# Ternary feed-forward weights prepared in the last batch's attention, and the last pairs' ends interleaved with the first feed-forward rows

## The chip, the cores and the metric

The kernel runs on one core of one Trainium2 chip. The metric is device time in microseconds (us) of one execution. The engines are PE (TensorE, matmuls), DVE (VectorE), ACT (ScalarE), POOL (GpSimd) and SP (SyncE, which here issues all DMAs). Each engine works through its own instructions in order; between engines only semaphores order the work.

## The reference

A transformer layer in fp32: differential attention after a layer norm, then a feed-forward block with ternary weights after a second layer norm, both with a residual. Batch 8, sequence 1024, width 512, 16 heads of 32, hidden width 2048.

```python
x = x + attn(layernorm(x))
# attn: q, k, v = (x @ w_qkv) in 16 heads of 32, q and k split into halves of 16
a = softmax(q1 k1 * s) - lam * softmax(q2 k2 * s)
out = rmsnorm(a @ v) * norm_w * 0.2          # then reshaped (heads * seq, 32) -> transposed -> (seq, 512)
return out @ wo

x = x + ffn(layernorm(x))
def bitlinear(x, w):                          # ffn
    scale = clip(mean(abs(w), axis=1), 1e-5)
    tern = clip(round(w / scale), -1, 1)
    return x @ (tern * scale).T
h = bitlinear(x, w_fc) + gate * (x @ v.T @ fast_b.T @ u.T)
return bitlinear(relu(h) ** 2, w_proj)
```

## The kernel before

**Attention.** Work goes by pairs of heads: 8 batches of 8 pairs, P = 0 to 63 (`NPAIR`). A pair has 16 tiles, 8 for each of the two softmaxes (j = 0, 1), and one turn of the inner loop (d = 0 to 7) handles two tiles. For a tile PE computes scores in two halves (`pe_score`, L530, PSUM banks 0-1 and 2-3), ACT takes the exponential of each (`act_exp`, L863) into a ring of four tiles `pr`, PE multiplies them with V (`pe_pv`, L557), and DVE adds the tile to `acc` (`dve_add`, L1156, none for the first tile of each eight). A half's scores wait for the exponential of the same half one tile before; an exponential waits until the tile four before it is added and multiplied. `pe_sum` (L574) turns `acc` into row sums; ACT makes their inverse with a logarithm and an exponential (`act_sum_ln` L869, `act_sum_exp` L873).

**Ends of pairs.** What is left of a pair after its tiles is cut into steps (`pe_post`, `act_post`, `dve_post`, `sync_post`), which ride along with the next three pairs: step 1 `ot` (DVE L1169, L1172), 2 its square (ACT), 3 the mean square by matmul into bank 5 (PE L589, `rms`), 4 its inverse root (ACT L889, L892) and `on` (DVE L1179), 7 transposes and their split `oth`, `otl` (PE L599, ACT L897, DVE L1183), 13 the load of the pair's rows of x into `xr` (SP L353), 14 and 15 twelve matmuls with `wo` into bank 7 (PE L610), 16 the addition `xr` (DVE L1188) and its write to `x2_scratch` (SP L357). There is one `xr`: the load of a pair's rows waits until the pair before has been written.

**Projections.** While batch b attends, the matmuls `x @ w_qkv` of a later batch run in pieces within its pairs (`pe_tile`, L469). For the last batch, pairs 56 to 63, nothing is left to project.

**Seam.** After pair 63 the ends of the last three pairs run down (loops such as L413, L775, L977 and L1303). Then, when the last rows are written (`s_x2` at 16 x 64), the feed-forward weights are prepared in eight slices, four of `w_fc` and four of `w_proj`. For each slice: SP loads 1 MB into `wf` (three slots; the first three loads are issued at the end of pair 55), ACT sums magnitudes (`act_magnitudes`, L908), DVE forms scales and compares against plus and minus half a scale (`dve_ternary`, L1205 to L1219) into `tt`, PE transposes 16 blocks through all eight banks (`pe_ternary`, L683), ACT copies them into `tT` or `tP` (`act_ternary`, L916). Between slices 4 and 5 the low-rank weights `w2s` are formed from `u`, `fast_b` and `v` (L1310 to L1337, `pe_low_rank_weights` L692 to L707, with 32-row casts L1333 and L1331). Then follow the layer norm of the first 512 rows (`dve_ln_step`, L1033 to L1055), the row of projection scales `prow` (PE L794, DVE L1349), the transposes of the rows (`pe_turn_rows` L661, ACT L922, DVE L1385), and `pe_low_rank` (L669).

**Feed-forward.** 16 blocks of 512 rows, 16 steps in each: `pe_up` (L629, L634), ACT relu (L1009), DVE square (L1360), ACT rounding (L1014), DVE remainder (L1362), `pe_down` (L644).

**Order.** The order on every engine is written out by hand. SBUF: in the seam, buffers of the feed-forward lie over those of attention, which is why its work starts after the last pair.

Of the kernel before, what the change touches and what calls it, by code (L numbers as in the profile page):

```python
# [31 lines left out]
STG = 8  # L32
# [12 lines left out]

def tile_of(m):
    return 2 * m if m < 4 else 2 * (m - 4) + 1
# [19 lines left out]
def build(nc, x, wqkv, wo, lq1, lq2, lk1, lk2, norm_w, fast_b, w_fc, w_proj, u, v, gate, out):  # L67
# [6 lines left out]
    with ExitStack() as top:  # L74
# [12 lines left out]
        scp = sbuf(top, "scp", [128, 4, 4])  # L87
        eps5, eps6, neglam, gatec = small[:, 0:1], small[:, 1:2], small[:, 2:3], small[:, 3:4]
        dt_ = small[:, 8:16]

        g1 = top.enter_context(ExitStack())
        with ExitStack() as al:
            wf = sbuf(al, "wf", [128, 3, HID])
            ta = sbuf(al, "ta", [128, 2, HID])
        wqh = sbuf(g1, "wqh", [128, 4, 3 * E], FR)
        wql = sbuf(g1, "wql", [128, 4, 3 * E], FR)
        woh = sbuf(g1, "woh", [128, 4, E], FR)
        wol = sbuf(g1, "wol", [128, 4, E], FR)
# [29 lines left out]
        with ExitStack() as al:  # L128
            pr = sbuf(al, "pr", [128, NPB, 2, 2, 512])
        with ExitStack() as al:  # L130
            wst = sbuf(al, "wst", [128, 4, 3 * E])
        with ExitStack() as al:
            stp = sbuf(al, "stp", [128, STG, 2, 512], FR)
        wos = acc[:, 0, :].rearrange("p (k n) -> p k n", k=4)
        g1.close()

        g2 = top.enter_context(ExitStack())
        with ExitStack() as al:
            zt = sbuf(al, "zt", [128, 2, 512], FR)
            zq = sbuf(al, "zq", [128, 512], FR)  # L140
            rb = sbuf(al, "rb", [128, 2, 512])
            sb2 = sbuf(al, "sb2", [128, 2, 512])
            hh_ = sbuf(al, "hh_", [128, 3, 512], FR)
            hl_ = sbuf(al, "hl_", [128, 3, 512], FR)
            fo = sbuf(al, "fo", [128, 4, E])
        sbuf(g2, "wf_place", [128, 3, HID])
        sbuf(g2, "ta_place", [128, 2, HID])
        tT = sbuf(g2, "tT", [128, 4, HID], FR)
        tP = sbuf(g2, "tP", [128, 16, E], FR)
        w2s = sbuf(g2, "w2s", [128, HID], FR)  # L150
        vth = sbuf(g2, "vth", [128, 4, 128], FR)
        vtl = sbuf(g2, "vtl", [128, 4, 128], FR)
        prow = sbuf(g2, "prow", [128, E])
        x2 = sbuf(g2, "x2", [128, 2, 4, E])
        xn = sbuf(g2, "xn", [128, 4, E])
        mv2 = sbuf(g2, "mv2", [128, 4, 2])
        st62 = sbuf(g2, "st62", [128, 4, 6])
        rs2 = sbuf(g2, "rs2", [128, 16])
        ln2 = sbuf(g2, "ln2", [128, 24])
        with ExitStack() as al:  # L160
            tt = sbuf(al, "tt", [128, 2, HID])
            us = sbuf(al, "us", [128, 16, RANK])
            ut = sbuf(al, "ut", [128, 2, 128])
            fba = sbuf(al, "fba", [128, 128])
            fbm = sbuf(al, "fbm", [128, 8, 128])
            vrep = sbuf(al, "vrep", [128, E])
            w2t = sbuf(al, "w2t", [128, 512], FR)
            dg = sbuf(al, "dg", [128, 4, 128])
            on1 = sbuf(al, "on1", [128, 128])
        with ExitStack() as al:  # L170
            yh = sbuf(al, "yh", [128, 2, 4, 512], FR)
            yl = sbuf(al, "yl", [128, 2, 4, 512], FR)
# [1262 lines left out]
```

## Time and profile before

| | |
|---|---|
| time, median of 3 runs | 4001.5 us (3999.47 to 4004.07) |
| profiled execution | 4001.55 us, span 3999.8 us |
| busy in the span | PE 3826.3 us (96%), DVE 3197.0 (80%), ACT 2834.5 (71%), POOL 2.0 |
| granted PE clock, whole execution | 0.987 |
| chain that ended last, by engine | PE 79%, DVE 10%, ACT 6%, issue 3%, DMA 1%, SP queue 1% |

The page shows the span in 40 slices of 100 us. PE, ACT and DVE are at nine, eight and nine tenths from the second slice on; slice 29 has PE and DVE at eight, ACT at four and the clock at six tenths; from slice 30 on PE is at nine, DVE at five, ACT at three. The tables of the page and the answers of the trace are read for where an engine idles and what ended its wait, since a busy share alone is an average over stages.

### The profile page before, as it was taken

To read this page: it belongs to the slowest core of one execution; us is meant where nothing else is said; L and a number is where in the kernel's file an instruction comes from. 1 tells how busy PE (TensorE), PEld (TensorE's weight loads), DVE (VectorE), ACT (ScalarE), POOL (GpSimd) and SP (SyncE) were. 2 spreads that over 40 slices of the span, in tenths; PEclk is the share of its full clock that TensorE was granted. 3 is DMA by queue.
4 is the path that set the end of the run, shared out by engine and by line. 5 is a ranking of instruction groups with operands and counts; after the bars stand their busy time and mean duration, and the time that the engine had idled before them with its cause. 6 is when DMAs were issued, how large, how long until landed. Compare 5 with 4: busy or idle time off the path is not lost.

```text
span 3999.8 us, 57643 instructions
## 1 busy us (share of the span) xinstructions
PE 3826.3 (96%) x22088; PEld 2113.7 (53%) x22088; DVE 3197.0 (80%) x3030; ACT 2834.5 (71%) x3573; POOL 2.0 (0%) x14
## 2 busy tenths in 40 slices
PE   6799999999999999999999999888499999999999
PEld 5344444444444444444444444232378787878887
DVE  5699999999999999999999999999655555555554
ACT  2688888888888888888888888888433333333333
POOL 0000000000000000000000000000000000000000
PEclk9899999999999999999999999999699999999999
DMA  5445444454454444444444545331201010101010
GB/s 196 123 100 117 101 111 111 94 124 98 111 109 100 115 108 109 107 104 110 107 111 103 111 97 125 63 67 38 90 6 38 22 42 22 43 22 43 22 43 22
DMA packets 225844, 338.25 MB, mean 85 GB/s; under 512 B 86704, under 2 KB 107184, under 8 KB 225008
## 3 DMA queue, kind: packets, MB, share of 16 engines
q1 hardware_dynamic: 225520, 333.88, 34.4%
q8 instruction: 210, 3.44, 0.4%
q14 instruction: 114, 0.93, 0.1%
HBM read 180.72 MB, written 150.99 MB: 83 GB/s over the span
## 4 chain that ended last, share of the span: by engine, by line
PE 79%; DVE 10%; ACT 6%; issue 3%; DMA 1%; SPq 1%; DVEq 0%; ACTq 0%
PE ps L557 18%; PE ps L530 13%; PE ps L629 12%; PE ps L644 12%; DVE acc L1156 7%; PE ps L469 7%; PE ps L472 5%; PE ps L610 4%; ACT pr L863 4%; PE ps L574 3%; PE ps L634 2%; PE ps L589 1%; PE ps L445 1%; PE ps L669 1%; PE ps L661 1%
## 5 line engine op out<-in xcount | busy, mean ns | idle before, releaser
L863 ACT ACTIVATE pr<-ps 128x1024 f32<-128x1024 f32 x2048 | 1983.9, 1027 | 248.8 <-PE ps L530 244.2
L1156 DVE TENSOR_TENSOR acc<-acc,pr 128x2048 f32<-128x2048 f32 x768 | 1755.4, 2286 | 55.2 <-ACT pr L863 27.8
L557 PE MATMUL ps<-pr,vst 128*32 128x512 f32 x8192 | 1021.2, 600 | 0.0
L530 PE MATMUL ps<-qst,kst 50*128 50x512 f32 x4096 | 786.0, 456 | 55.4 <-ACT pr L863 37.8
L530 PEld LDWEIGHTS ps<-qst,kst 50*128 50x128 f32 x4096 | 329.7, 184 | 721.7 <-ACT pr L863 534.6
L1009 ACT ACTIVATE rb<-ps,scf 128x512 f32<-128x512 f32 x256 | 175.9, 687 | 407.1 <-PE ps L634 407.1
L557 PEld LDWEIGHTS ps<-pr,vst 128*32 128x32 f32 x8192 | 207.9, 109 | 439.9 <-issue 429.8
L629 PE MATMUL ps<-yh,tT 128*128 128x512 f32 x1024 | 410.4, 401 | 0.0
L644 PE MATMUL ps<-tP,hh_ 128*128 128x512 f32 x1024 | 406.2, 397 | 1.9 <-DVE hl_ L1362 1.9
L629 PE MATMUL ps<-yl,tT 128*128 128x512 f32 x1024 | 405.3, 396 | 0.0
L1360 DVE TENSOR_TENSOR sb<-rb 128x512 f32<-128x512 f32 x256 | 176.9, 691 | 282.9 <-ACT rb L1009 281.6
L644 PE MATMUL ps<-tP,hl_ 128*128 128x512 f32 x1024 | 401.2, 392 | 0.0
L1156 DVE TENSOR_TENSOR acc<-pr 128x2048 f32<-128x2048 f32 x128 | 293.0, 2289 | 104.4 <-ACT pr L863 104.4
L1362 DVE TENSOR_TENSOR hl_<-sb,hh_ 128x512 fp32r<-128x512 f32 x256 | 177.2, 692 | 178.9 <-ACT hh_ L1014 178.9
L1014 ACT ACTIVATE hh_<-sb 128x512 fp32r<-128x512 f32 x256 | 162.0, 633 | 202.5 <-DVE sb L1360 202.5
L469 PE MATMUL ps<-xth,wqh 128*128 128x512 f32 x512 | 223.1, 436 | 9.7 <-DVE stg L1089 9.7
L644 PEld LDWEIGHTS ps<-tP,hh_ 128*128 128x128 f32 x1024 | 192.3, 188 | 60.4 <-DVE fo L1396 12.5
L629 PEld LDWEIGHTS ps<-yh,tT 128*128 128x128 f32 x1024 | 192.6, 188 | 43.2
L629 PEld LDWEIGHTS ps<-yl,tT 128*128 128x128 f32 x1024 | 192.6, 188 | 42.9
L644 PEld LDWEIGHTS ps<-tP,hl_ 128*128 128x128 f32 x1024 | 192.3, 188 | 42.8
L469 PE MATMUL ps<-xtl,wqh 128*128 128x512 f32 x512 | 205.9, 402 | 0.0
L469 PE MATMUL ps<-xth,wql 128*128 128x512 f32 x512 | 202.6, 396 | 0.0
(154 smaller groups left out, 3500.8 us busy)
## 6 DMA issues: line engine op xcount, KB each, us to landing
qst<-q_scratch SPq DMA_DIRECT2D x128, 384.0 KB, 6.3
kst<-k_scratch SPq DMA_DIRECT2D x128, 384.0 KB, 9.1
q_scratch<-stg SPq DMA_DIRECT2D x168, 256.0 KB
k_scratch<-stg SPq DMA_DIRECT2D x168, 256.0 KB
xin<-in_L_attn_x_dram SPq DMA_DIRECT2D x16, 1024.0 KB, 5.7
v_scratch<-vsg SPq DMA_DIRECT2D x64, 256.0 KB, 3.0
vst<-v_scratch SPq DMA_DIRECT2D x128, 128.0 KB, 5.5
xr<-in_L_attn_x_dram SPq DMA_DIRECT2D x64, 256.0 KB
```

The costliest lines, as they stand in the source:

```text
L469: t = e.matmul(ps[:, bk, :], w[:, k, m0:m0 + 128], xx[:, k, :], start=(n == 0), stop=(n == 11))
L472: t = e.matmul(ps[:, bk, :], xx[:, k, st * 128:(st + 1) * 128], w[:, k, 2 * E:3 * E], start=(n == 0), stop=(n == 11))
L530: ins = e.matmul(ps[:, 2 * c + hh, :], kst[rows, r, j, t * 128:(t + 1) * 128], qst[rows, r, j, c * 512:(c + 1) * 512], start=True, stop=True)
L557: ins = e.matmul(ps[32 * c4:32 * c4 + 32, 4 + j, :], vst[:, r, t, 32 * hh:32 * hh + 32], pr[:, sl, c, hh, :], start=(t == 0), stop=(t == 7 ...
L629: e.matmul(ps[:, bk, :], tT[:, k, i * 128:(i + 1) * 128], y_[:, bf, k, :], start=(m == 0), stop=False)
L644: t = e.matmul(ps[:, rt, :], h_[:, uu % 3, rt * 128:(rt + 1) * 128], tP[:, i, :], start=(i == 0 and part == 0), stop=(i == 15 and part == 1))
L863: e.activation(pr[:, sl, c, :, :], ps[:, 2 * c:2 * c + 2, :], ACT.Exp, scale=SCALE).then_inc(s_exp, 1)
L1009: e.activation(rb[:, uu % 2, :], ps[:, 4 + uu % 2, :], ACT.Relu, scale=scf[:, 0, i:i + 1]) \
L1014: e.activation(hh_[:, uu % 3, :], sb2[:, uu % 2, :], ACT.Copy).then_inc(s_hh, 1)
L1156: e.tensor_tensor(acc[:, j, :], old, new, ALU.add).then_inc(s_add, 1)
L1360: e.tensor_tensor(sb2[:, uu % 2, :], rb[:, uu % 2, :], rb[:, uu % 2, :], ALU.mult).then_inc(s_sb, 1)
L1362: e.tensor_tensor(hl_[:, uu % 3, :], sb2[:, uu % 2, :], hh_[:, uu % 3, :], ALU.subtract) \
```

## The change

- SBUF is laid out anew. The feed-forward's weights, work buffers and constants (`tT`, `tP`, `tt`, `ta`, `wf`, now with two slots, `us`, `fba`, `vrep`) lie over the projections' buffers (`wqh` to `vsg`), which are free once the last projections are done; the row buffers (`x2`, `xn`) lie over `pr`, `yh` over `acc`, `yl` over `qst`.
- Slice i of the weights is handled in pair 56 + i: magnitudes at d = 0, 2, 3 (ACT), scales and first comparison at d = 4, second comparison at d = 5 and 6 (DVE, two pieces each), transposes and copies at d = 6, 7 and d = 0, 1 of the next pair (PE, ACT), all through bank 6. Every slice is now in four pieces of 512 columns; for `w_proj` a `tensor_reduce` adds the four magnitude sums.
- SP loads slices 0 and 1 at the end of pair 55, `u`, `fast_b` and `v` at d = 1 of pair 56, and one slice at d = 7 of each of pairs 56 to 61. `u` is scaled by DVE at d = 0 of pair 62.
- After pair 63 the order on each engine is written out: the last pairs' ends stand between the low-rank weights, the scales and the layer norm of the first rows. `pe_sum` of the last pair uses bank 3. Rows 0 to 1023 are loaded without waiting for the last batch's writes. ACT rounds all of `w2s` in one instruction a block, so DVE's casts of 96 of the 128 rows go.
- The twelve `wo` matmuls of pair 63 stand in the feed-forward behind its first down step, its addition two steps later.

```diff
@@ SP
+                    if d == 1 and P == NPAIR - NP:
+                        sync_low_rank(e)
+                    if d == 7 and NPAIR - NP <= P < NPAIR - 2:
+                        sync_weights(e, P - (NPAIR - NP) + 2)
                     sync_posts(e, P, d)
-            for d in range(24):
-                sync_posts(e, NPAIR + d // 8, d % 8)
-            e.wait_ge(s_x2, 16 * NPAIR)
...
+            sync_post(e, NPAIR - 3, 16)
             sync_rows(e, 0)
+            sync_post(e, NPAIR - 2, 13)
             sync_rows(e, 1)
...
+            sync_post(e, NPAIR - 2, 16)
+            sync_post(e, NPAIR - 1, 13)
+            sync_post(e, NPAIR - 1, 16)
@@ PE
                     pe_posts(e, P, d)
+                    if last and d >= 6:
+                        pe_ternary(e, P - (NPAIR - NP), d - 6)
+                    if last and d < 2 and P > NPAIR - NP:
+                        pe_ternary(e, P - (NPAIR - NP) - 1, d + 2)
...
+            pe_pv(e, NSLOT - 3)
+            pe_pv(e, NSLOT - 2)
+            pe_ternary(e, 7, 2)
+            pe_pv(e, NSLOT - 1)
+            pe_ternary(e, 7, 3)
+            pe_post(e, NPAIR - 2, 14)
+            pe_post(e, NPAIR - 2, 15)
+            pe_low_rank_factors(e)
+            pe_sum(e, NPAIR - 1, 1)
+            pe_low_rank_weights(e, 0)
+            pe_low_rank_weights(e, 1)
+            pe_row_scales(e)
+            pe_post(e, NPAIR - 1, 3)
+            pe_low_rank_weights(e, 2)
+            pe_low_rank_weights(e, 3)
             for k in range(4):
                 pe_turn_rows(e, 0, k)
+            pe_post(e, NPAIR - 1, 7)
             pe_low_rank(e, 0)
...
+                    if n == 0 and i == 1:
+                        pe_post(e, NPAIR - 1, 14)
+                        pe_post(e, NPAIR - 1, 15)
@@ PE, one transpose bank
+        def pe_ternary(e, i, m):
+            u4 = 4 * i + m
+            e.wait_ge(s_tern, u4 + 1)
+            if u4:
+                e.wait_ge(s_tt, u4)
+            else:
+                tile_read(e, 24 * B - 1)
+            for k in range(4):
+                t = e.transpose(ps[:, 6, k * 128:(k + 1) * 128], tt[:, (4 * m + k) * 128:(4 * m + k + 1) * 128], ident[:])
+            t.then_inc(s_ttr, 1)
@@ ACT
                     act_exp(e, P, k, 0)
+                    if d in (0, 3) and tile >= 0:
+                        act_magnitudes(e, tile, 2 if d else 0)
...
+                    if d in (2, 3) and tile >= 0:
+                        act_magnitudes(e, tile, 2 * d - 3)
                     act_posts(e, P, d, 1)
+                    if d >= 6 and tile >= 0:
+                        act_ternary(e, tile, d - 6)
+                    if d < 2 and tile >= 1:
+                        act_ternary(e, tile - 1, d + 2)
                     act_exp(e, P, k + 1, 1)
@@ DVE
+                        tile = P - (NPAIR - NP)
+                        if tile >= 0 and (d, half) == (4, 0):
+                            dve_ternary_scale(e, tile)
+                        if tile >= 0 and (d, half) in ((5, 1), (6, 0)):
+                            for a in range(2):
+                                dve_ternary(e, tile, 2 * (d - 5) + a)
+                        if tile == 6 and (d, half) == (0, 0):
+                            dve_low_rank_u(e)
                         dve_add(e, P, 2 * d + half)
...
+            dve_post(e, NPAIR - 3, 16, 0)
             e.wait_ge(s_fb, 16 * 12)
+            e.wait_ge(s_pv, NSLOT)
...
+            dve_post(e, NPAIR - 1, 1, 0)
+            dve_post(e, NPAIR - 2, 16, 0)
             e.wait_ge(s_vta, 1)
...
+            dve_low_rank_weights(e, 0)
+            dve_low_rank_weights(e, 1)
+            e.wait_ge(s_w2p, 5)
+            e.tensor_copy(prow[:], ps[:, 1, :]).then_inc(s_prow, 1)
+            for n in range(5):
+                dve_ln_step(e, 2 * B, n)
+            dve_low_rank_weights(e, 2)
+            dve_low_rank_weights(e, 3)
+            dve_post(e, NPAIR - 1, 4, 1)
             for n in range(6, 11):
                 dve_ln_step(e, 2 * B, n)
...
             for k in range(4):
                 dve_turn_rows(e, 0, k)
+            dve_post(e, NPAIR - 1, 7, 1)
             dve_low_rank(e, 0)
```

## Rows read from the trace of the kernel before

**Rows 1.** Busy time by stretch (us): stretch, length, each engine's busy time (instructions), PE clock, DMA.
```profile
2394.81:2436.26 41.45, 41.45 (x266) 18.64 (x264) 39.12 (x27) 36.74 (x44) 0.00 (x0) 1.00 0.49 117
2676.28:2716.08 39.80, 35.71 (x232) 11.88 (x228) 36.18 (x21) 34.48 (x41) 0.00 (x0) 1.00 0.31 62
2812.26:2920.09 107.83, 49.16 (x233) 40.02 (x234) 64.69 (x141) 40.73 (x84) 0.84 (x3) 0.67 0.26 83
2920.09:3992.00 1071.91, 1069.50 (x4708) 857.03 (x4707) 565.87 (x964) 398.80 (x634) 0.00 (x0) 1.00 0.09 29
```

**Rows 2.** Waits in the pair 2676.28 to 2716.08: total us, times, longest.
```profile
DVE acc L1156 <- ACT pr L863: 2.0, 5, 1.1
...
DVE otl L1183 <- ACT oth L897: 0.4, 1, 0.4
...
DVE ot L1169 <- ACT rl L873: 0.2, 1, 0.2
```

**Rows 3.** Order of time in that pair, ACT and PE: start, length (us), engine, line.
```profile
2701.11 3.79 ACT L863 ACTIVATE pr<-ps 128x1024 f32<-128x1024 f32 x4
2705.09 1.94 ACT L863 ACTIVATE pr<-ps 128x1024 f32<-128x1024 f32 x2 [0.20 <-PE ps L530]
2706.37 1.13 PE L589 MATMUL ps<-sq,blk 128*128 128x256 f32 x4
2707.97 1.94 ACT L863 ACTIVATE pr<-ps 128x1024 f32<-128x1024 f32 x2 [0.94 <-PE ps L530]
...
2710.37 1.95 ACT L863 ACTIVATE pr<-ps 128x1024 f32<-128x1024 f32 x2
```

**Rows 4.** Order of time on DVE in the seam, weight preparation and first layer norm.
```profile
2849.19 0.16 DVE L1205 TENSOR_SCALAR scf<-scf 128x4 f32<-128x4 f32 x1
...
2853.90 0.16 DVE L1205 TENSOR_SCALAR scf<-scf 128x4 f32<-128x4 f32 x1
...
2870.52 2.30 DVE L1318 TENSOR_SCALAR us<-us,scf 128x16 f32<-128x16 f32 x16
...
2903.97 2.46 DVE L1033 BATCH_NORM_STATS2 st<-x 128x6 f32<-128x512 f32 x4
...
2908.05 1.92 DVE L1055 TENSOR_SCALAR xn<-x,mv,rs 128x512 f32<-128x512 f32 x4
```

**Rows 5.** Order of time on ACT in the seam, magnitudes and copies.
```profile
2851.24 0.62 ACT L908 ACTIVATE ta<-wf 128x512 f32<-128x512 f32 x1
...
2851.86 2.03 ACT L916 ACTIVATE tT<-ps 128x512 fp32r<-128x512 f32 x4
```

**Rows 6.** Order of time on DVE and SP, end of attention, the last rows' rounds.
```profile
2809.97 2.29 DVE L1156 TENSOR_TENSOR acc<-acc,pr 128x2048 f32<-128x2048 f32 x1 [0.23 <-ACT pr L863]
...
2812.89 0.55 SPq L357 DMA_DIRECT2D x_scratch<-xr  x1
2818.79 0.57 SPq L353 DMA_DIRECT2D xr<-in_L_attn_x_dram  x1
...
2832.24 0.55 SPq L353 DMA_DIRECT2D xr<-in_L_attn_x_dram  x1
...
2837.53 0.69 DVE L1188 TENSOR_TENSOR xr<-ps,xr 128x512 f32<-128x512 f32 x1 [11.18 <-DMA xr<-in_L_attn_x_dram]
...
2844.09 0.17 DVE L1205 TENSOR_SCALAR scf<-scf 128x4 f32<-128x4 f32 x1 [5.87 <-DMA x_scratch<-xr]
```

**Rows 7.** Order of time on PE in the seam, first transposes of weights and rows, the low-rank product.
```profile
2854.04 1.97 PE L683 MATMUL ps<-ident,tt 128*128 128x128 f32 x16 [1.01 <-DVE tt L1219]
...
2910.62 1.76 PE L661 MATMUL ps<-ident,xn 128*128 128x128 f32 x8 [1.91 <-DVE prow L1349]
...
2916.51 0.80 PE L669 MATMUL ps<-yh,vth 128*128 128x512 f32 x1 [1.41 <-DVE yl L1385]
...
2920.09 0.63 PE L629 MATMUL ps<-yh,tT 128*128 128x512 f32 x1
```

**Rows 8.** Line L366, the two loads of 1 MB of rows in the seam.
```profile
DMA to landing us min/median/max: 7.1/8.0/9.0
```

More of the change, by code:

```diff
@@ new lines, in build @@
+            mv2 = sbuf(al, "mv2", [128, 4, 2])
+            st62 = sbuf(al, "st62", [128, 4, 6])
+            rs2 = sbuf(al, "rs2", [128, 16])
+            ln2 = sbuf(al, "ln2", [128, 24])
+        with ExitStack() as al:
+            w2s = sbuf(al, "w2s", [128, HID], FR)
+            zt = sbuf(al, "zt", [128, 2, 512], FR)
+            zq = sbuf(al, "zq", [128, 512], FR)
+            prow = sbuf(al, "prow", [128, E])
+            hh_ = sbuf(al, "hh_", [128, 3, 512], FR)
+            vth = sbuf(al, "vth", [128, 4, 128], FR)
+            hl_ = sbuf(al, "hl_", [128, 3, 512], FR)
+            vtl = sbuf(al, "vtl", [128, 4, 128], FR)
@@ L99, in build @@
+        with ExitStack() as al:
+            wst = sbuf(al, "wst", [128, 4, 3 * E])
+        with ExitStack() as al:
+            stp = sbuf(al, "stp", [128, STG, 2, 512], FR)
+        pr = sbuf(g1, "pr", [128, NPB, 2, 2, 512])
+        acc = sbuf(g1, "acc", [128, 2, 2 * S])
         qst = sbuf(g1, "qst", [128, RING, 2, S], FR)
@@ L183, in build @@
         s_vb = [sem(f"s_vb{k}") for k in range(RING)]
-        s_wf = [sem(f"s_wf{k}") for k in range(3)]
+        s_wf = [sem(f"s_wf{k}") for k in range(2)]
         s_u, s_fb = sem("s_u"), sem("s_fb")
@@ L1224, in build @@
-        dve_count = [0]
+            e.wait_ge(s_abs, 4 * i + 4)
+            if not fc:
+                e.tensor_reduce(scp[:, 3, cols], scq[:, i - 4, :], AX.X, ALU.add).then_inc(s_scl, 1)
+                c += 1
+                e.wait_ge(s_scl, c)
+            e.tensor_scalar(sc[:, 0, cols], sc[:, 3, cols], 1.0 / (512 if fc else 2048), 1e-5, ALU.mult, ALU.max) \
+                .then_inc(s_scl, 1)
+            e.wait_ge(s_scl, c + 1)
+            e.tensor_scalar(sc[:, 1, cols], sc[:, 0, cols], 0.5, None, ALU.mult).then_inc(s_scl, 1)
@@ new lines, in dve_ternary_scale, with dve_ternary @@
+            e.tensor_scalar(sc[:, 2, cols], sc[:, 0, cols], -0.5, None, ALU.mult).then_inc(s_scl, 1)
+            e.wait_ge(s_scl, c + 3)
+            for a in range(4):
+                _, col, cs = wf_part(i, a)
+                e.tensor_scalar(ta[:, cs], wf[:, i % 2, cs], sc[:, 2, col:col + 1], None, ALU.is_lt).then_inc(s_scl, 1)
+        def dve_ternary(e, i, a):
+            sc, col, cs = wf_part(i, a)
+            if i:
+                e.wait_ge(s_ttr, 4 * i)
+            e.wait_ge(s_scl, n_scale(i + 1) - 3 + a)
+            e.scalar_tensor_tensor(out=tt[:, cs], in0=wf[:, i % 2, cs], scalar=sc[:, 1, col:col + 1], in1=ta[:, cs],
+                                   op0=ALU.is_gt, op1=ALU.subtract).then_inc(s_tern, 1)
@@ new lines, in dve_low_rank_u @@
+        def dve_low_rank_u(e):
+            e.wait_ge(s_scl, n_scale(4))
+            e.reciprocal(scf[:, 1, :], scf[:, 0, :]).then_inc(s_lru, 1)
+            e.wait_ge(s_lru, 1)
+            e.wait_ge(s_small, 16 * 9)
+            e.tensor_scalar(scf[:, 2, :], scf[:, 1, :], gatec, None, ALU.mult).then_inc(s_lru, 1)
+            e.wait_ge(s_lru, 2)
+            e.wait_ge(s_u, 16)
+            for t in range(16):
+                ins = e.tensor_scalar(us[:, t, :], us[:, t, :], scf[:, 2, t:t + 1], None, ALU.mult)
+            ins.then_inc(s_w2v, 1)
```

383 lines of the change are left out of this document (154 added, 229 removed).

## Prediction

> **What bounds the kernel now.** I read the page first. Three engines are busy over 70% of the span, so the shares decide nothing, and the slices show what matters: PE, ACT and DVE are dense over 27 slices, thin out in slices 28 and 29, and then PE alone is dense to the end. I then cut the time into stretches [rows 1]. A pair of attention heads with projection matmuls in it takes 41.45 us, and PE is busy for all of it. A pair of the last batch, which has no projections left, takes 39.80 us with PE 35.7, DVE 36.2 and ACT 34.5 busy. The seam from the end of the last addition to `acc` (the addition of 2809.97 lasts 2.29, so it ends at 2812.26 [rows 6]) to the first matmul of the feed-forward (2920.09 [rows 7]) is 107.8 us, with no engine over 60% busy and a granted PE clock of 0.67, a mixture of the 1.2 and the 2.4 GHz level. After it PE is busy 1069.5 of 1071.9 us. So the seam is the loose stretch, the last batch has a little room, and the feed-forward has none: a matmul more there costs its full pitch.
>
> In a last-batch pair no single engine sets the pace. DVE's waits are 2.0 for the exponentials, 0.4 and 0.2 for the ends of earlier pairs, 2.6 us in all [rows 2]. What paces it is the ring between ACT and PE: a half tile of exponentials frees the PSUM banks for the next scores, and the next exponential waits for those. ACT's order of time shows it [rows 3]: two plain tiles take 3.98 us (2701.11 to 2705.09), 1.99 each; the tile with the `rms` matmuls in it takes 2.88, the one with a logarithm 2.40. PE's extra (1.13 us busy, some 1.0 of it added) passes with 0.89 into the period; ACT's extra, about 0.6 us as for any instruction of 512 columns there, with 0.41.
>
> **Part 1: ternary preparation moved into the last eight pairs.** Each pair takes one of eight slices. DVE: in the seam one slice of `w_fc` took from 2849.19 to 2853.90, 4.71 us [rows 4]. A slice of `w_proj` has four pieces now and one small sum more; I take 4.7 for both. ACT: four magnitudes at 0.61 (one starts at 2851.24, what follows at 2851.86) and four copies in 2.03, so 4.5 us [rows 5]. PE: 16 transposes in 1.97 us [rows 7]. What this does to a pair of 39.80:
> - DVE's floor: 39.8 less its waits of 2.6, plus 4.7, is 41.9.
> - ACT's load is 34.5 + 4.5 = 39.0, PE's at most 35.7 + 2.0 = 37.7. Neither is a bound alone.
> - The ring: the transposes stand between two score matmuls, so I pass them on as the `rms` matmuls are (0.89 of 1.97, 1.75 us). Magnitudes pass at ACT's rate (0.41 of 0.6 of 2.46, 1.7 us). The copies stand directly behind transposes, where PE issues the next scores at the same time; that hides them nearly fully (0 to 0.68 x 2.03 = 1.4). The ring is then 43.2 to 44.6.
>
> The bounds: below, the DVE floor (it can't be less, as every piece is issued by DVE in order); above, 44.5, all of DVE's present waits kept and 4.7 added; a ring that hides nothing would give 39.8 + 2.0 + 4.5 = 46.3. I take 43.4, near the low end of the ring since ACT and PE both have 4 us of room, and above the floor: +3.6 a pair, +28.8 over eight. The scaling of the `u` factors, also moved in, is 2.3 us of DVE once [rows 4], and two small instructions ahead of it make it about 2.8; DVE has 43.4 - 41.9 = 1.5 of room by then, so +1.3 (0 to 2.8). Together **+30.1** (17 to 40).
>
> Where the waits could hurt: PE's transposes of a slice wait for DVE's masks, and behind them in PE's queue stand the scores of the next half tile, for which ACT waits, and then DVE. By the order in the code the mask pieces come before the additions of tiles 11 and 12 and the first transposes after the scores of tile 13, so DVE has two additions (4.6 us) in hand when PE starts; a wait there drains nothing. SP gets 13 small loads in the first of these pairs and one weight load in six, each behind that pair's K, Q and V loads; those are issued a pair ahead, and I cost them at nothing. Without that cover they would cost some 7 us once, at about 0.5 us for each as for SP's issues in the seam.
>
> **Part 2: the seam.** From the end of the last addition (t = 0), by the new order:
> - Pair 61's rows are added and written at 0.7. Its write takes from 2812.89 to 2818.79 before SP can load pair 62's rows, 5.9 us, and a load 5.2 (2832.24, then DVE at 2837.53) [rows 6]. So pair 62's addition, now in the middle of DVE's queue, can't start before 11.8. Meanwhile PE has pair 62's 12 projection matmuls, the transposes of `u` and `v`, the last sum and the first low-rank matmuls; ACT and DVE turn the last pair's sums into `ot`. I count this to 9 us: covered.
> - A load of 1 MB of rows is now issued between that write and that load. The two such loads together landed after 7.1 and 9.0 us, median 8.0 [rows 8]. I add 1 us: DVE goes on at 12.8.
> - The Trainium skill, DMA: Bandwidth & Descriptors, section Queues, rings and completion order, says that on each DMA engine the descriptors of one ring are consumed in order. By that pair 62's load would wait for what is left of the 1 MB, and were that load to take its 8.0 us here, from 1.3 to 9.3, pair 62's rows would come 2.7 us after the 11.8 of free engines, not 1.
> - Then DVE alone: the addition, `vth`, four roundings of `w2s`, `prow`, `on`: eight instructions in all, most of them as long as the addition itself (0.69 [rows 6]), 5.2 us; and the layer norm of the first rows, 2903.97 to 2909.97 (1.92 after 2908.05 [rows 4]), 6.0 us, of which about 0.8 is `dg`, which moves ahead: 5.2. Together 10.4: t = 23.2.
> - From the first transposes of those rows to the first feed-forward matmul: 2910.62 to 2920.09, 9.5 us [rows 7], as now. The last pair's four transposes fall into PE's wait before 2916.51. t = 32.8.
>
> So 107.8 becomes **33**, -74.8. Gone are: the wait for the last pair's write and read round (DVE waits of 11.18 and 5.87 us [rows 6]), eight slices of preparation, and 12 of 16 casts of `w2s`. What is late next is DVE's chain with pair 62's rows in it. Bounds: 31 without the added microsecond and with DVE's pieces back to back, 38 if each of some ten hand-overs between DVE, ACT and PE costs 0.5 more.
>
> The low-rank matmuls of the tail show the slow clock: eight from 2916.51 to 2920.09 are 0.45 us each, where the feed-forward has 1071.9 us for 4708, 0.228 each [rows 1, 7]. PE stands idle for longer than 1 us ahead of them in the new order too, so I keep 0.45. The Trainium skill, TensorE: Matmul & The Clock Gate, section Part 1, holds that activity releases the throttle; should the denser seam do that, the seam would be 8 x 0.22 = 1.8 us shorter.
>
> **Part 3: the end of the last pair within the feed-forward.** Its 12 projection matmuls stand behind the first down step: 12 x 0.228 = **+2.7**, since PE has no room there (0 to 2.7: pipeline gaps of the first steps might take some). DVE's one addition there is covered: DVE is busy 566 of 1072 us [rows 1]. The write of pair 63 is waited for only by the rows of the last batch, far later.
>
> **Sum**: the profiled execution took 4001.55 (span 3999.8), its median 4001.5. 4001.55 + 30.1 - 74.8 + 2.7 = 3959.5, say **3960**.
>
> **The rivals.**
> A, the preparation hides down to DVE's floor. For it: the projection pair, where a saturated PE makes ACT's and DVE's extras vanish. 8 x 2.1 + 2.8 = 19.6 in place of 30.1: **3949**.
> B, it hides nowhere: DVE's waits are by order and stay, 4.7 a pair and 2.8: 40.4, **3970**. For it: the ring has waits on both sides already [rows 2].
> C, the seam is gated by memory: if the first rows' layer norm ends up behind both remaining rounds of write and load (0.7 + 5.9 + 5.2 + 0.7 + 5.9 + 5.2 = 23.6, and then as above), the seam is 44: **3970**. Against it: the rows of the first batch don't depend on those pairs, and SP's queue has their loads ahead of the last round.
> D, on the other side: the in-order queues lock. PE waits for a mask of DVE, ACT for PE's transposes, DVE for ACT's exponentials, and each slice's steps lie in series with the pair's: 4.7 + 2.0 + 2.0 + 2.5 = 11.2 a pair, 92.2 with `u`: **4022**. It becomes slower than before from 9.0 us a pair on, (74.8 - 2.7) / 8. Against it: the two additions in hand worked out above.
> E, the change doesn't take the preparation off the path: some wait (buffers over `wqh`, the one transpose bank) bunches it behind the last pair; about 4000.
>
> **How the numbers follow.** Chances: forecast 0.50, A 0.17, B 0.16, C 0.10, D 0.04, E 0.03. The range goes from a little below A (floor, a seam of 31 and nothing for part 3: 3944) to B with 6 us for the longer seam: 3944 to 3976. About 0.2%, 8 us, is what a measurement of this kernel can tell from no change. Faster 0.93, within it 0.03, slower 0.04.
>
> **What would show it.** Right: pairs of the last batch at 43 to 44 us with DVE waiting about 1.5; the first feed-forward matmul about 33 us after the last addition; pair 62's addition at about 12.8 in that count, and released by its load; the feed-forward longer by 2 to 3 us. Wrong: pairs under 42 or over 45; masks (DVE) among PE's waits of the last batch; an engine's queue held by a load in the seam later than 13 us.

## The result and the profile after

| | before | after |
|---|---|---|
| time, median of 4 runs each on one chip | 4000.6 us (3999.5 to 4004.1) | 3933.6 us (3931.9 to 3933.9) |
| after / before, with 95% interval | | 0.983 (0.981 to 0.985) |
| profiled execution, span | 3999.8 us | 3932.1 us |
| granted PE clock, whole execution | 0.987 | 0.994 |

The change saves 67 us where 42 were forecast: the sign is right, the time lies 26 us below the prediction and 10 us below its range. The two spans, 67.7 us apart, are cut at the same places of the work:

| stretch | before | after | difference | forecast |
|---|---|---|---|---|
| start to pair 55's multiplication of `rl` (L1197, after: L1245), some 13 us ahead of the last batch | 2478.2 | 2477.5 | -0.7 | 0 |
| from there to the end of the last addition to `acc` | 334.1 | 355.6 | +21.5 | +30.1 |
| seam, to the first feed-forward matmul | 107.8 | 35.9 | -71.9 | -74.8 |
| feed-forward, to the end of the span | 1079.7 | 1063.1 | -16.6 | +2.7 |

The largest miss is in the stretch that the prediction thought it could count best: the feed-forward should have become 2.7 us longer and became 16.6 shorter, 19.3 us apart.

The busy time by stretch of the kernel after, in the columns of [rows 1]: a pair of the last batch (cut as in [rows 1], from one such multiplication of `rl` to the next, that is from the middle of one pair to the middle of the next), the seam, and the feed-forward up to 3924.

```profile
2602.99:2645.47 42.48, 38.09 (x244) 13.66 (x244) 40.09 (x32) 38.65 (x53) 0.00 (x0) 1.00 0.38 82
2833.08:2869.01 35.93, 20.61 (x94) 15.78 (x94) 18.32 (x46) 9.81 (x19) 0.20 (x1) 0.74 0.33 88
2869.01:3924.00 1054.99, 1052.89 (x4718) 859.68 (x4717) 565.03 (x965) 399.14 (x634) 0.00 (x0) 1.00 0.09 30
```

The pair takes 42.48 us for 39.80 before: +2.7, not +3.6. The seam has 94 matmul records for 233, since the preparation stands in the pairs now. And the third line holds more matmuls than its counterpart (4718 for 4708) in 17 us less: PE was saturated before and after, so each matmul follows the one before it sooner.

The waits within that pair of the kernel after (total us, times, longest), answering [rows 2]:

```profile
PE ps L541 <- ACT pr L905: 4.3, 10, 0.6
ACT oth L939 <- PE ps L614: 1.8, 1, 1.8
...
DVE acc L1204 <- ACT pr L905: 1.5, 1, 1.5
```

DVE waits 1.5 for the exponentials, as forecast; no mask of DVE is among PE's waits. ACT in the same pair, answering [rows 3] and [rows 5]: start, length, line; L905 is the exponential, L952 the magnitudes.

```profile
2629.46 1.97 ACT L905 ACTIVATE pr<-ps 128x1024 f32<-128x1024 f32 x2
2631.27 0.68 ACT L952 ACTIVATE ta<-wf 128x512 f32<-128x512 f32 x1
...
2631.88 1.99 ACT L905 ACTIVATE pr<-ps 128x1024 f32<-128x1024 f32 x2
2633.69 0.70 ACT L952 ACTIVATE ta<-wf 128x512 f32<-128x512 f32 x1
...
2634.30 2.00 ACT L905 ACTIVATE pr<-ps 128x1024 f32<-128x1024 f32 x2
2636.11 0.71 ACT L952 ACTIVATE ta<-wf 128x512 f32<-128x512 f32 x1
...
2636.95 1.94 ACT L905 ACTIVATE pr<-ps 128x1024 f32<-128x1024 f32 x2
```

The starts of the exponentials are the pace. A tile with a magnitude takes 2.42 us (2629.46 to 2631.88, and again to 2634.30): 0.43 over the plain tile's mean of 1.99 of before, close to the 0.41 that the prediction read off the tile with a logarithm. The third, 2634.30 to 2636.95, holds a magnitude and the four `rms` matmuls, and takes 2.65, where `rms` alone made it 2.88 before. The two extras don't add up.

The seam of the kernel after, SP's issues, which answer [rows 6] (L369 write, L365 load of a pair's rows of x, L383 load of 1 MB of the feed-forward's rows):

```profile
2833.71 0.55 SPq L369 DMA_DIRECT2D x_scratch<-xr  x1
2834.37 0.41 SPq L383 DMA_DIRECT2D x<-x_scratch  x1
2841.20 0.59 SPq L365 DMA_DIRECT2D xr<-in_L_attn_x_dram  x1
2841.91 0.41 SPq L383 DMA_DIRECT2D x<-x_scratch  x1
```

And its DVE and PE in order of time, answering [rows 4] and [rows 7]:

```profile
2849.08 0.69 DVE L1236 TENSOR_TENSOR xr<-ps,xr 128x512 f32<-128x512 f32 x1 [7.76 <-DMA xr<-in_L_attn_x_dram]
...
2857.48 1.92 DVE L1103 TENSOR_SCALAR xn<-x,mv,rs 128x512 f32<-128x512 f32 x4
```

```profile
2859.45 1.97 PE L692 MATMUL ps<-ident,xn 128*128 128x128 f32 x8 [5.21 <-DVE xn L1103]
...
2865.43 0.80 PE L702 MATMUL ps<-yh,vth 128*128 128x512 f32 x1 [0.56 <-DVE yl L1444]
2866.02 0.63 PE L702 MATMUL ps<-yl,vth 128*128 128x512 f32 x1
2866.45 0.63 PE L702 MATMUL ps<-yh,vth 128*128 128x512 f32 x1
...
2869.01 0.63 PE L652 MATMUL ps<-yh,tT 128*128 128x512 f32 x1
```

The last addition ends at 2833.08. Pair 61's write takes 7.5 us (2833.71 to 2841.20; 5.9 before), pair 62's load 7.9 until DVE starts (5.3 before, 2832.24 to 2837.53), and DVE stands 7.76 us in front of pair 62's addition, which is late at 16.0. From there the chain is as forecast: DVE 10.3 us to 2859.40, PE 9.6 us to 2869.01.

### The profile page after: what moved, and what is told of

Read it like the earlier page. It is cut to its first block, busy times and chain, and to the rows that moved or that the text cites. A ratio compares the mean times of both kernels' runs of the same rounds, so it can differ in the third digit from the quotient of the medians.

```text
span 3932.1 us, 57774 instructions
## 1 busy us (share of the span) xinstructions
PE 3799.9 (97%) x22088; PEld 2106.5 (54%) x22088; DVE 3184.3 (81%) x3046; ACT 2835.5 (72%) x3597; POOL 2.0 (0%) x14
## 4 chain that ended last, share of the span: by engine, by line
PE 80%; DVE 10%; ACT 6%; issue 3%; DMA 1%; SPq 1%; DVEq 0%; ACTq 0%
PE ps L568 18%; PE ps L541 13%; PE ps L672 12%; PE ps L652 12%; DVE acc L1204 8%; PE ps L480 7%; PE ps L483 5%; PE ps L628 4%; ACT pr L905 4%; PE ps L589 3%; PE ps L657 1%; PE ps L604 1%; PE ps L456 1%; PE ps L702 1%; PE ps L692 1%
## 5 line engine op out<-in xcount | busy, mean ns | idle before, releaser
L905 ACT ACTIVATE pr<-ps 128x1024 f32<-128x1024 f32 x2048 | 1988.7, 1029 | 225.5 <-PE ps L541 220.8
L672 PE MATMUL ps<-tP,hh_ 128*128 128x512 f32 x1024 | 404.3, 395 | 1.9 <-DVE hl_ L1419 1.9
L652 PE MATMUL ps<-yh,tT 128*128 128x512 f32 x1024 | 404.9, 395 | 0.0
L652 PE MATMUL ps<-yl,tT 128*128 128x512 f32 x1024 | 399.9, 391 | 0.0
L672 PE MATMUL ps<-tP,hl_ 128*128 128x512 f32 x1024 | 399.1, 390 | 0.0
L672 PEld LDWEIGHTS ps<-tP,hh_ 128*128 128x128 f32 x1024 | 192.1, 188 | 56.8 <-DVE fo L1457 12.5
L652 PEld LDWEIGHTS ps<-yl,tT 128*128 128x128 f32 x1024 | 192.8, 188 | 39.0
L652 PEld LDWEIGHTS ps<-yh,tT 128*128 128x128 f32 x1024 | 192.8, 188 | 38.5
L672 PEld LDWEIGHTS ps<-tP,hl_ 128*128 128x128 f32 x1024 | 192.3, 188 | 37.7
```

The costliest lines, as they stand in the source:

```text
L652: e.matmul(ps[:, bk, :], tT[:, k, i * 128:(i + 1) * 128], y_[:, bf, k, :], start=(m == 0), stop=False)
L672: t = e.matmul(ps[:, rt, :], h_[:, uu % 3, rt * 128:(rt + 1) * 128], tP[:, i, :], start=(i == 0 and part == 0), stop=(i == 15 and part == 1))
L905: e.activation(pr[:, sl, c, :, :], ps[:, 2 * c:2 * c + 2, :], ACT.Exp, scale=SCALE).then_inc(s_exp, 1)
```

## The experiments

### The feed-forward: where yh and yl lie

The page's costliest groups (busy us, mean ns of one) show where the matmuls became shorter. Before:

```profile
L629 PE MATMUL ps<-yh,tT 128*128 128x512 f32 x1024 | 410.4, 401 | 0.0
L644 PE MATMUL ps<-tP,hh_ 128*128 128x512 f32 x1024 | 406.2, 397 | 1.9 <-DVE hl_ L1362 1.9
```

After:

```profile
L672 PE MATMUL ps<-tP,hh_ 128*128 128x512 f32 x1024 | 404.3, 395 | 1.9 <-DVE hl_ L1419 1.9
L652 PE MATMUL ps<-yh,tT 128*128 128x512 f32 x1024 | 404.9, 395 | 0.0
```

The means fall by 6 ns for the up matmuls (L629, after: L652) and by 2 for the down matmuls (L644, L672); 4352 matmuls are of this size. The wait in front of them is the same, and the instructions are too. What differs is where the operands lie in SBUF: `tT`, `tP`, `w2s`, `hh_`, `hl_` and `zt` stood at 224 modulo 512 bytes before and `yh`, `yl` at 0; after the new layout all eight stand at 288. The first theory, A, was that the rows `yh`, `yl` and the weights `tT` must have the same offset modulo 64 bytes; its rival B put the gain on the region of SBUF, on any shift or on the order of work. The first test moved `yh` and `yl` alone, by an unused buffer ahead of them. Four more are the same edit with other sizes: b_y64 16 columns, b_y96 24, b_y224 56, b_y480 120; the number in a name is the offset of `yh` and `yl` modulo 512 bytes.

```diff
             # b_y32, on the kernel before
+            sbuf(al, "gap", [128, 8])
             yh = sbuf(al, "yh", [128, 2, 4, 512], FR)
```

> The kernel before, with an unused 32 bytes per partition ahead of yh, so that yh and yl start at 32 modulo 64 bytes, as every other tile that the feed-forward's matmuls read already does. Theory A (the feed-forward became 19 us shorter because the moving rows yh, yl no longer lie at another offset within 64 bytes than the weights tT): matmuls of L629 start every 227 ns instead of 231 to 236, the down matmuls behind them too, the feed-forward from its first matmul to the end takes about 1060 us instead of 1080, the time is 3981 (3978 to 3985). Theory B (the shortening is due to which SBUF region each tile lies in, or to the order of work): no change, 4000 within 3 us.

> The kernel before, with an unused 64 bytes ahead of yh: yh and yl move, but stay at 0 modulo 64. Theory A (offset within 64 bytes): no change, 4000, pitch pattern 231 to 241 ns as before. Theory B (any shift away from a multiple of 512 bytes, or of the region, helps): 3981.

In the kernel after the same shift goes the other way, `yh` and `yl` 32 bytes off the rest (a_y32; `sb2` and `fo`, which no matmul reads, move along); and all large tiles can be shifted together (a_all32).

```diff
             # a_y32, on the kernel after
-            sbuf(al, "gap", [128, 128])
+            sbuf(al, "gap", [128, 136])
             # a_all32, on the kernel after, behind scq
+        sbuf(top, "pad", [128, 8])
```

> The kernel after, with its gap ahead of yh 32 bytes longer: yh, yl, sb2 and fo start at 0 modulo 64, the weights stay at 32. Theory A: the up matmuls are back at 231 to 236 ns and the feed-forward is about 19 us longer, time 3952 (3949 to 3956). Theory B: 3934 within 3 us.

> The kernel after, with an unused 32 bytes ahead of all large tiles, so that yh, yl, tT, tP, hh_ and hl_ all start at 0 modulo 64 and none at 32. Theory A1 (what counts is that weights and moving rows have the same offset within 64 bytes): no change, 3934. Theory A2 (a moving operand at 0 modulo 64 is slow by itself): all feed-forward matmuls at 231 ns or more, 20 to 35 us longer, 3954 to 3969.

> The kernel before, with an unused 224 bytes ahead of yh, so that yh and yl lie at 224 modulo 512 bytes, exactly where tT, tP, w2s, hh_ and hl_ lie. With 32 bytes the first four to seven matmuls of a step were still at 229 to 237 ns. Theory A3 (for the steady 227 ns the offsets must be the same modulo 512, or at least modulo 128 or 256): all 17 positions of a step at a median of 227, the feed-forward 19 us shorter than before, time 3981 (3978 to 3985). Theory A (only the offset within 64 bytes counts, the rest is the order of work): as with 32 bytes, 3990.

> The kernel before, with an unused 96 bytes ahead of yh: yh and yl at 96 modulo 512, the same as tT's 224 modulo 128 but not modulo 256. Theory A3 for 128 bytes: all positions of a step at 227 ns and 3982, as with 224 bytes. Theory A3 for 256 or 512 bytes: the first positions of a step are still disturbed, as with 32 bytes, 3988 to 3992.

> The kernel before with a gap of 120 columns ahead of yh: yh and yl then lie at 480 modulo 512 bytes, all other tiles of the feed-forward at 224. That is the same offset modulo 256, another modulo 512. With yh and yl at 224 the feed-forward, from its first up matmul to its last matmul, took 1054.0 us, with them at 0 it took 1073.0. Theory modulo 512: 1062 to 1076 us and some up matmuls at 231 to 241 ns. Rival modulo 256: 1054 us and 227 ns for every matmul of a step. I hold the first at 0.6, as 96 (the same modulo 128) gave 1066.4.

The last one moves `tT` away and leaves everything that streams through PE where it is.

```diff
             # b_tT, on b_y224
+        sbuf(g2, "pad1", [128, 8])
         tT = sbuf(g2, "tT", [128, 4, HID], FR)
+        sbuf(g2, "pad2", [128, 120])
```

> The kernel before with yh and yl at tT's old offset (224 modulo 512 bytes) and then tT alone moved by 32 bytes, to 256; tP, w2s, zt, hh_, hl_, yh and yl all stay at 224. The up matmuls then have their weights (tT) and their rows (yh, yl) at different offsets, while the operands that stream through one after another (yh, yl, zt, hh_, hl_) keep one. Theory that weights and rows of a matmul must agree: the up matmuls at 231 to 241 ns, the feed-forward at 1064 to 1076 us. Rival, that the tiles streamed one after another must agree: 227 ns everywhere, 1054 us.

Measured, worked out from the start times of the matmuls in each trace: the feed-forward from the start of its first up matmul to the start of its last matmul (of the kernels after, 2.7 us are the twelve `wo` matmuls), and the median of start to next start, in ns, at the 17 places of a step, 8 up, 1 low-rank, 8 down. The offset is that of the rows (`yh`, `yl`) minus that of the weights `tT`, modulo 256.

```
kernel   offset  feed-forward  up                               low-rank  down
before       32  1073.0        236 231 236 234 231 235 233 234  241       224 231 236 229 232 231 227 227
b_y32        64  1062.7        236 235 232 232 226 229 231 226  229       232 231 227 227 227 227 227 227
b_y64        96  1073.2        236 233 235 232 240 233 237 232  231       231 236 228 232 231 227 227 227
b_y96       128  1066.4        234 224 237 229 237 229 237 229  232       233 231 227 227 227 227 227 227
b_y224        0  1054.0        227 everywhere
b_y480        0  1054.0        227 everywhere
b_tT        224  1066.3        231 229 235 232 235 232 235 233  231       227 227 227 227 227 227 227 235
after         0  1056.4 - 2.7  227 everywhere
a_y32        32  1075.7 - 2.7  236 231 235 234 231 235 233 234  241       224 231 235 229 232 231 227 227
a_all32       0  1056.2 - 2.7  227 everywhere
```

The times: b_y32 3989.8 us, 0.9973 (0.9964 to 0.9983) of before; b_y224 3982.6, 0.9954 (0.9937 to 0.9970), so 18 to 19 of the 67 us by the medians for a buffer of 224 bytes a partition that holds nothing (the interval allows 12 to 25, the feed-forward's own 19.0 is the sharper figure); a_y32 3952.1, 0.9879 (0.9862 to 0.9895), which gives 18.5 of them back. By single executions b_y64 took 3998.3, b_y96 3996.7, b_y480 3981.4, b_tT 3990.4, a_all32 3935.0.

What follows:
- Theory A is wrong. By it b_y32 would have won it all, and it won 10 of 19 us. So is B: the shift of b_y64 wins nothing (1073.2), and the one of b_y224, in the same region and order, everything. In a_all32 the tiles move from 32 to 64 modulo 256 together and nothing changes. It is no property of one tile; it is the relation between tiles.
- The kernel after with the offset of before (a_y32, 32 apart) repeats the pattern of before to 1 ns at every place, and its 1073.0 us. This takes every other difference between the kernels out of the question.
- Modulo 128 is not enough (b_y96), modulo 256 is (b_y480). I held modulo 512 at 0.6, and that was wrong. For b_y96 I had expected 3988 to 3992 us; it took 3996.7.
- b_tT separates two readings of "relation". A matmul holds one operand as weights and streams the other. `tT` (up), `w2s` (low-rank) and `hh_`, `hl_` (down) are weights; `yh`, `yl`, `zt` and, in the down matmuls, `tP` stream. What streams has one offset in b_tT, and of the weights only those of the up matmuls differ. Its groups:

```profile
L632 PE MATMUL ps<-yh,tT 128*128 128x512 f32 x1024 | 410.5, 401 | 0.0
L647 PE MATMUL ps<-tP,hh_ 128*128 128x512 f32 x1024 | 404.2, 395 | 1.9 <-DVE hl_ L1365 1.9
```

The up matmuls have their 401 ns of before, the down matmuls their 395 of after. So it is weights against what streams. Since the loading of the next weights lies under the streaming of the present matmul (PEld is busy 860 us within PE's 1053), the weights may be those of the matmul or of the next one. The 235 ns at the last down matmul of b_tT, whose successor loads `tT`, speaks for the next one. The up matmuls of b_tT fit both. No run separates that further, and why it costs something isn't shown by any record.

### The last batch: what sets a pair's 42.5 us

Theory R was a ring between ACT and PE; rivals were a floor of DVE (D, and F in the last of these), and P, by which PE hides most of its transposes in its own waits. Each run takes most of one engine's addition away and leaves the others.

```diff
             # a_dve: first comparison (L1268) on 16 of 512 columns
+                cs = slice(cs.start, cs.start + 16)
             # a_act: magnitudes on 16 of 512 columns
-            cs = wf_part(i, a)[2]
+            cs = slice(512 * a, 512 * a + 16)
             # a_pe: one transpose of four
-            for k in range(4):
+            for k in range(4 if u4 == 0 else 1):
             # a_both: a_act, and a_dve's edit from slice 1 on
```

> The kernel after with the first comparison of the ternary weights made on 16 of each 512 columns (the rest of the mask is stale, so the weights are not the reference's): DVE has about 1.0 us less in each of the last eight pairs, ACT and PE the same. Theory D (DVE's own sum paces the last pairs, 42.5 us): pairs at 41.4 to 41.7, time 3925 to 3928. Theory R (the ring of PE and ACT paces them, as the prediction had it): pairs at 42.4 to 42.5, time 3933.

> The kernel after with the magnitudes summed over 16 of each 512 columns (scales are then too small and the weights not the reference's): ACT has about 1.6 us less in each of the last eight pairs, DVE and PE the same. Theory D: pairs at 42.2 to 42.5, time 3931 to 3934. Theory R: each pair 1.0 us or more shorter, time 3925 or less.

> The kernel after with one transpose in place of four for each group of the ternary weights but the first (the weights are then not the reference's): PE has about 1.3 us less in each of the last eight pairs, ACT and DVE the same. The prediction's step (PE's extras pass with 0.89 into the period): pairs 1.2 us shorter, 41.3, or at DVE's floor of 41.9, so time 3924 to 3929. Theory P (PE's transposes are mostly absorbed by PE's own waits for ACT, only the two groups that stand behind wo matmuls, where ACT waits for PE, pass): pairs 0.3 to 0.6 us shorter, DVE's floor 41.9 in the way, time 3929 to 3931.

> The kernel after with both cuts at once, magnitudes on 16 of 512 columns and, from the second slice on, the first comparison on 16 of 512 columns (weights not the reference's). Magnitudes alone gave pairs of 41.87 us. Theory F (there DVE's own sum of 41.9 had become the limit): pairs at 40.9 to 41.2, time 3918 to 3921. Rival (PE's ring is the limit there): pairs stay at 41.8, time 3925 to 3926.

The pair at the same place as above, busy time by stretch, first a_dve, then its wait of DVE for the exponentials:

```profile
2602.06:2644.53 42.47, 38.11 (x248) 13.66 (x244) 39.45 (x32) 38.65 (x53) 0.00 (x0) 1.00 0.38 82
```

```profile
DVE acc L1204 <- ACT pr L905: 2.0, 3, 1.6
```

DVE was relieved of 0.64 us (39.45 for 40.09; I had expected 1.0) and waits 0.5 longer; the pair stays at 42.47. DVE doesn't set the pace of this pair. Then a_act, a_pe and a_both:

```profile
2598.87:2640.74 41.87, 37.80 (x244) 13.59 (x244) 40.09 (x32) 37.10 (x54) 0.00 (x0) 1.00 0.38 83
```

```profile
2603.60:2645.73 42.13, 36.87 (x232) 12.42 (x232) 40.10 (x33) 38.64 (x53) 0.00 (x0) 1.00 0.37 83
```

```profile
2599.94:2641.82 41.88, 37.85 (x248) 13.58 (x244) 39.33 (x31) 37.08 (x53) 0.00 (x0) 1.00 0.36 83
```

ACT's load fell by 1.55 us and the pair by 0.61, a share of 0.39; PE's by 1.2 and the pair by 0.35, a share of 0.29. Both share in the ring, neither is it alone, and most of either addition is absorbed. P's 0.3 to 0.6 for a_pe was right; a_act missed both forecasts (0 to 0.3 by D, 1.0 or more by R). By the starts of the exponentials the five pairs 57 to 61 of each run agree within 0.04 us, so these differences are no scatter. Tile by tile, a_act gains 0.42, 0.41 and 0.42 us in the three tiles that hold a magnitude and nothing else, and gives back 0.41 in the tile with `rms` and 0.33 in the one behind the first magnitude; all of a_pe's gain stands in one tile, the one with the first transposes of a slice (3.90 to 3.57). a_both is a_act to 0.01 us in this pair, so here the floor isn't DVE's with ACT's load gone.

In the last two pairs it is, once ACT is relieved. The scaling of the `u` factors falls into the first of these intervals of the kernel after (43.65 us, the next 41.34), and from 2730.57 on DVE waits only 0.2 us in 85:

```profile
2730.57 0.68 DVE L1245 TENSOR_TENSOR rl<-ps,rl 128x512 f32<-128x512 f32 x1
...
2774.22 0.68 DVE L1245 TENSOR_TENSOR rl<-ps,rl 128x512 f32<-128x512 f32 x1
...
2815.56 0.68 DVE L1245 TENSOR_TENSOR rl<-ps,rl 128x512 f32<-128x512 f32 x1
```

The same two intervals sum to 85.0 us in a_act and in a_pe too, and to 83.7 in a_both. From pair 56's first exponential to the last addition the kernels take 342.3 (after), 342.0 (a_dve), 340.9 (a_pe), 338.9 (a_act) and 336.9 us (a_both): with ACT's load gone DVE's is worth 2.0 us there, nearly all of it in the last two pairs. The totals (3933.4, 3926.2, 3933.3, 3927.4 us) carry a scatter of up to 3.5 us from the part ahead of the last batch: pair 55's multiplication of `rl` stands anywhere from 2475.0 to 2478.5 in these runs; the pairs are compared for that reason.

### The seam: the order of SP's queue

The two loads of 1 MB stand between the small writes and loads on which DVE waits. In a_rows the first is issued ahead of pair 61's write, at 2826.92, and has landed 5.9 us later, before that write starts; the second is issued behind pair 63's load.

```diff
-            sync_post(e, NPAIR - 3, 16)
             sync_rows(e, 0)
+            sync_post(e, NPAIR - 3, 16)
             sync_post(e, NPAIR - 2, 13)
-            sync_rows(e, 1)
             sync_post(e, NPAIR - 2, 16)
             sync_post(e, NPAIR - 1, 13)
+            sync_rows(e, 1)
             sync_post(e, NPAIR - 1, 16)
```

> The kernel after, with the first rows' load issued ahead of pair 61's write, and the second rows' load behind the load of pair 63's rows. Theory C (in the seam pair 62's rows come late because both loads of 1 MB share the DMA engines with that write and load: 7.5 us and 7.9 us in place of 5.9 and 5.2): the write takes 5.9 and the load 5.2 again, pair 62's addition starts 11.9 us after the last addition to acc and not 16.0, the seam is 31.8 us and not 35.9, time 3929.5 (3928 to 3932). Rival (they are that slow because of their own access pattern or of what DVE does): 3933.6, same seam.

It took 3929.3 us (3928.8 to 3930.7), 0.9821 (0.9804 to 0.9837) of before; its runs and those of after (3931.9 to 3933.9) don't overlap, 4.3 us apart at the medians. The two were run beside different runs of before (medians 4001.6 and 4000.6), and the ratios' intervals overlap; that the gain is real rests on the traces, where the span is 4.6 us shorter and the seam 5.3. SP, DVE and PE of a_rows:

```profile
2826.92 0.37 SPq L383 DMA_DIRECT2D x<-x_scratch  x1
2834.35 0.54 SPq L369 DMA_DIRECT2D x_scratch<-xr  x1
2840.29 0.59 SPq L365 DMA_DIRECT2D xr<-in_L_attn_x_dram  x1
```

```profile
2846.01 0.69 DVE L1236 TENSOR_TENSOR xr<-ps,xr 128x512 f32<-128x512 f32 x1 [4.06 <-DMA xr<-in_L_attn_x_dram]
```

```profile
2862.34 0.50 PE L702 MATMUL ps<-yh,vth 128*128 128x512 f32 x1 [0.56 <-DVE yl L1444]
2862.68 0.39 PE L702 MATMUL ps<-yl,vth 128*128 128x512 f32 x1
2862.91 0.39 PE L702 MATMUL ps<-yh,vth 128*128 128x512 f32 x1
...
2864.29 0.39 PE L652 MATMUL ps<-yh,tT 128*128 128x512 f32 x1
```

The write takes 5.9 again (2834.35 to 2840.29) and the load 5.7. The last addition ends at 2833.71 there, so pair 62's addition stands at 12.3 instead of 16.0 (expected 11.9), and the seam is 30.6 us (expected 31.8). 3.7 of the 5.3 us gained are the two transfers; the other 1.6 are the low-rank matmuls, which start every 0.23 us at a granted clock of 1.00, the 2.4 GHz level, instead of every 0.43 at 0.50, the 1.2 GHz level. These 1.6 were in no expectation, so that the time came out at the 3929.5 expected is in part luck.

Last, a_rows with all large tiles at the offset of `ident` modulo 256, to see whether the slower matmuls behind each group of row transposes (for instance 231 236 228 233 231 226 227 ns) go with the same rule.

```diff
+        sbuf(top, "pad", [128, 88])
```

> The kernel after with the rows' loads in the new order and 352 unused bytes ahead of the large tiles, so that these lie at the same offset modulo 512 as ident (128), the operand of all transposes. Theory A3 says that in the after kernel the ten matmuls behind each group of transposes are slow because ident lies at another offset: with it they start every 227 ns, which is 2.6 to 3 us in the feed-forward and up to 4 us in the projections' pairs, time 3922 to 3927. Rival (the disturbance behind transposes comes from the transposes themselves): 3929.3 as with the new order of loads alone.

It took 3928.5 us (3925.3 to 3930.1), 0.9818 (0.9802 to 0.9835), not to be told from a_rows; the slower matmuls behind the transposes are all there, and the mean pitch is 227.6 ns for 227.8. This offset at least doesn't remove them, and I had expected 3922 to 3927 us of it. a_rows is the version to keep: it moves two calls and is faster than the kernel after.

## Why the prediction was wrong, step by step

**The bound.** Right in kind: no engine alone sets the pair, PE alone sets the feed-forward. The step that failed is in the sentence "the feed-forward has none", no room: it took the pitch itself for fixed. The prediction had 0.228 us for a matmul (1071.9 by 4708), but 240 of the 4708 are transposes of 128 columns, 0.11 us each; the 4352 of full size started 232.6 ns apart on the average. No part of its sum looked at where operands lie. The change moves every buffer of the feed-forward, and this part was costed at nothing, without a row looked at. It was worth -19.3 us, three quarters of the 25.7 by which the profiled execution missed its sum of 3959.5; without it that execution would have taken 3953.2, inside the range. (Of the 40 slices, the 29th, where the seam lies, has PE at four tenths and DVE at six, not both at eight; nothing in the sum hangs on that.) The trace of before had the sign of it: starts 231 to 241 ns apart in one place of a step and 227 in another, for matmuls of one shape in a saturated queue.

**Part 1, +30.1 forecast, +21.5 measured.** The term that was mis-sized is the ring. Compared tile by tile between the exponentials' starts, a pair grew by 2.67 us (forecast 3.6): 1.24 in the four tiles with magnitudes (forecast 1.7), 1.43 in those with transposes and copies (forecast 1.75 for the transposes and 0 to 1.4 for the copies). Two steps failed. The passing share 0.89 of PE's extras was taken from one place, where `rms` stands alone against ACT; a_pe shows 0.29. And extras of PE and ACT were added in series: where both fall into one tile they lie side by side (2.65 us with magnitude and `rms`, 2.88 with `rms` alone, 3.07 in a_act). ACT's extras were to pass with 0.41 us of 0.6, a share of 0.68. In the plain tiles that held (0.43), for the pair it did not: a_act shows 0.39. DVE's floor of 41.9 was too high: in the interval of 41.34 us after the one with `u`, where DVE waits 0.2, it needs 41.1 for a pair and its slice. That a_act's pairs, 41.87, fall on 41.9 is chance; DVE waits 0.9 in them. The `u` factors, forecast 1.3, cost at most 0.5: the interval with them is 1.2 longer and the next 1.1 shorter, the exponentials go on every 42.5 us, and what is left is 0.5 between pair 63's first exponential and the last addition (45.43 us, for 42.24 before and 2.68 of its own slice).

**Part 2, -74.8 forecast, -71.9 measured.** Right: what goes, what is late next (DVE with pair 62's addition, released by its load), DVE's tail (10.3 for 10.4), PE's (9.6 for 9.5), the slow clock of the low-rank matmuls. Mis-sized: the collision with the 1 MB loads, 1 us in the sum, cost 1.6 on the write, which lay open from the first moment and wasn't counted, and 2.6 on the load (7.9 for 5.3; the prediction read 5.2 off the same rows). a_rows takes 3.7 of these away. The sentence on the Trainium skill, DMA: Bandwidth & Descriptors, Queues, rings and completion order, gave 2.7 us instead of 1 for waiting behind the first 1 MB, and stood nearer: 16.0 - 11.8 = 4.2. The trace agrees further: the first 1 MB landed at 2843.84, 2.64 us behind the load's issue, and the load took 2.6 longer. In the seven kernels with this order of issues DVE's addition comes 4.5 to 5.3 us behind that landing. It is no proof of in-order service, since the second 1 MB was issued 0.7 us behind the load and a_rows moved both; transfers that slow each other by sharing a rate could look the same. The 1.8 us that the prediction set on a released clock did not come in the kernel after (0.43 us each) and did in a_rows (1.6). PE idles 5.21 us ahead of its transposes in the one, 5.83 in the other, so what decides between the levels isn't shown; the Trainium skill, TensorE: Matmul & The Clock Gate, Part 1, would put it on activity, and no run here varied that alone.

**Part 3, +2.7 forecast, +2.7 measured.** The twelve matmuls in the feed-forward of the kernel after:

```profile
2877.39 0.39 PE L628 MATMUL ps<-woh,oth 128*128 128x512 f32 x1
...
2880.12 0.39 PE L652 MATMUL ps<-yh,tT 128*128 128x512 f32 x1
```

**The rivals.** A came nearest in time (3949), by luck: the last batch cost 21.5 and not 19.6, DVE's own sum sets at most the last two of its pairs, and what brought the time down was the feed-forward. C, a longer seam, happened in a small way, by colliding transfers and not by its own mechanism. D and E: no trace of them; no wait of PE for a mask stands among its waits of the last batch. (D's 92.2 is 92.4 by its own terms.) The range failed because all its ends were made from steps of the schedule; none had a case in which the steps that were not edited change their price.

**The sum again**, from 3959.5: feed-forward -19.3, last batch -8.6, seam +2.9, start -0.7: 3933.8, where the profiled execution took 3933.9.

## What to carry to other kernels

When a change moves buffers, ask what reads them at full rate, and compare the addresses of a matmul's weights and of its streamed operand modulo 256 bytes before and after: here that was over a quarter of the whole gain, and an unused buffer of 224 bytes had it without the rest. Look at the spacing of equal matmuls in a saturated stretch; if it isn't the same everywhere, there is something to win that no busy share shows. Extras of two engines in a ring shouldn't be summed, and a large load doesn't belong between two small transfers on which an engine waits.

## What the hardware showed that I had not expected

- fp32r matmuls of 128x512 with a weight load each start every 227 ns when the weights (`tT`, `w2s`, `hh_`, `hl_`) and the streamed operands (`yh`, `yl`, `zt`, `tP`) share one offset modulo 256 bytes; with the rows of the up matmuls 32 bytes off, every 224 to 241 ns; mean 227.8 against 232.6 ns, 19 of 1073 us. The size depends on the difference: 64 bytes cost 8.7 us, 32 and 96 cost 19, 128 cost 12.4.
- The disturbance outlasts its cause: behind the last mismatched matmul, up to six matched ones still start 224 to 236 ns apart, and four to nine behind each group of row transposes do so in nearly the same sequence.
- A write of 256 KB went from 5.9 to 7.5 us with a 1 MB load issued 0.7 us behind it, and a load of 256 KB from 5.3 to 7.9 with that 1 MB still in flight and a second one issued 0.7 us behind.
- In two kernels that differ in the place of two DMA calls, the same low-rank matmuls ran at the 1.2 GHz level (granted clock 0.50, 0.43 us each) in one and at the 2.4 GHz level (1.00, 0.23) in the other.
